# Queries projected transposed, with omega and the norm applied in 64x64 fp32 tiles, in a fused attention and expert layer

## The reference

```python
h = _layernorm(x) * (1 + ca) + sa
q = _heads(h @ wq.T); k = _heads(h @ wk.T); v = _heads(h @ wv.T)
def _phi(x, omega):                       # per head: D = 64 -> M = 64 features
    proj = jnp.einsum('bhnd,md->bhnm', x, omega)
    norm = 0.5 * jnp.sum(x * x, axis=-1, keepdims=True)
    return jnp.exp(proj - norm) / math.sqrt(M)
phi_q = _phi(q, omega); phi_k = _phi(k, omega)
# causal: out = phi_q . cumsum(phi_k v), z = 1 / (phi_q . cumsum(phi_k) + 1e-6)
out = (out * z[..., None]) @ wo.T + bo
...                                       # residual, norm, top-2 routing, experts
```

## Time and profile before

| | us |
|---|---|
| median of 3 executions | 726.92 (726.3 to 727.3) |
| the profiled execution | 727.18 |
| its span in the trace | 725.1 |
| PE busy | 697.4 (96% of the span) |
| DVE busy | 536.0 (74%) |
| ACT busy | 387.6 (53%) |
| POOL busy | 335.6 (46%) |

### The profile page before, as it was taken

One profiled execution on the slowest core, in us unless ns is written; L12 is line 12 of the kernel. 1 busy time (PEld: TensorE's weight loads), 2 busy tenths in 40 slices (PEclk: granted clock), 3 DMA queues, 4 the chain that ended last, 5 costly groups with the idle time before them and its releaser, 6 DMA issues. The chain is left out here.

```text
span 725.1 us, 27349 instructions
## 1 busy us (share of the span) xinstructions
PE 697.4 (96%) x11452; PEld 604.1 (83%) x11452; DVE 536.0 (74%) x1685; ACT 387.6 (53%) x740; POOL 335.6 (46%) x625
## 2 busy tenths in 40 slices
PE   8999999999999999999999999999999789999956
PEld 8788888888888888888888888888887779999942
DVE  6687888878878887888878878888775456565416
ACT  5755566665656665666656566665552144544310
POOL 3002545555544445454545554545447306556550
PEclk9999999999999999999999999999999999999989
DMA  9974000000000000000000000000000154553128
GB/s 252 362 268 178 11 9 11 10 9 11 14 15 10 11 10 11 10 10 11 9 11 11 14 14 9 11 11 11 10 11 14 49 177 130 168 173 113 51 82 304
DMA packets 32705, 47.25 MB, mean 65 GB/s; under 512 B 4132, under 2 KB 20168, under 8 KB 32584
## 3 DMA queue, kind: packets, MB, share of 16 engines
q1 hardware_dynamic: 23296, 32.62, 13.4%
q0 software_dynamic: 4096, 8.42, 3.6%
q10 hardware_dynamic: 5192, 4.47, 1.9%
HBM read 22.21 MB, written 23.36 MB: 63 GB/s over the span
## 5 line engine op out<-in xcount | busy, mean ns | idle before, releaser
L1297 POOL DMA_INDIRECT y_rows<-y_sb,row_id x64 | 62.8, 982 | 66.0 <-DVE y_sb L1442 49.9
L1108 POOL DMA_INDIRECT dispatched<-h_cur,slot x64 | 67.3, 1051 | 17.8 <-issue 16.1
L1376 ACT ACTIVATE hidden<-bank,b_col 128x512 f32<-128x512 f32 x64 | 43.3, 689 | 58.2 <-PE bank L1348 57.8
L632 ACT ACTIVATE phi_k<-expo_k 128x1024 f32<-128x1024 f32 x32 | 33.9, 1058 | 74.5 <-DVE expo_k L768 70.7
L648 ACT COPY v_sb<-bank 128x512 f32<-128x512 f32 x64 | 37.6, 587 | 62.1 <-PE bank L279 58.7
L527 PEld LDWEIGHTS bank<-woT,attT 128*128 128x128 f32 x512 | 61.9, 192 | 3.2 <-ACT attT L738 0.6
L859 DVE TENSOR_TENSOR scores<-bank,within 128x512 f32<-128x512 f32 x64 | 41.2, 686 | 31.2 <-PE bank L310 31.2
L527 PE MATMUL bank<-woT,attT 128*128 128x128 f32 x512 | 62.4, 275 | 0.4 <-ACT attT L738 0.4
L1317 PE MATMUL bank<-w_sb,hidden 128*128 128x128 f32 x512 | 59.7, 275 | 0.8 <-issue 0.8
L137 POOL TENSOR_TENSOR rs<-var,power 128x1 f32<-128x1 f32 x64 | 37.1, 579 | 49.8 <-DVE var L132 49.5
L1317 PEld LDWEIGHTS bank<-w_sb,hidden 128*128 128x128 f32 x512 | 58.3, 192 | 1.2 <-issue 1.2
(11 more groups left out here) (243 smaller groups left out, 2037.9 us busy)
## 6 DMA issues: line engine op xcount, KB each, us to landing
dispatched<-blank SPq DMA_DIRECT2D x16, 524.0 KB, 3.1
region<-dispatched SPq DMA_DIRECT2D x30, 262.0 KB, 2.9
y_rows<-blank SPq DMA_DIRECT2D x8, 512.0 KB, 3.9
w_nat<-in_L_ffn_w_dram SPq DMA_DIRECT2D x8, 256.0 KB, 3.7
y_got<-y_rows SPq DMA_DIRECT2D x8, 256.0 KB, 6.8
y_got<-y_rows ACTq DMA_DIRECT2D x8, 256.0 KB, 7.4
out_dram<-x_sb SPq DMA_DIRECT2D x8, 256.0 KB, 3.7
w_sb<-in_L_ffn_w_dram ACTq DMA_DIRECT2D x6, 256.0 KB, 2.8
```

The source lines that it names most:

```text
L1108: pool.indirect_dma_start(out=dispatched[:, :], in_=h2_cur[par][:], in_offset=None, out_offset=bass.IndirectOffsetOnAxis(ap=slot[par][:, k ...
L1297: pool.indirect_dma_start(out=y_rows[:, :], out_offset=bass.IndirectOffsetOnAxis(ap=row_id[par][:, t:t + 1].bitcast(U32), axis=0), in_=y_s ...
L1376: act.activation(hidden[par][:, k, :], psum[2 + k][:], ACT.Gelu, bias=b1_col[:, bass.ds(e * KH + k, 1)]).then_inc(sem(f"hid{k}_out"), 1)
```

## The change

Queries are projected with the weights stationary and 128 tokens moving, so that the result stands transposed (a head's dimensions on partitions): 24 fp32r matmuls of 128 columns for a chunk in place of 6 of 512. ACT copies this result to `qT` and its square to `qT_square`. PE then multiplies by omega and adds -0.5 times the sum of squares with 32 plain fp32 matmuls of 128 columns in 64x64 tiles (`exponent_qT`), and ACT takes the exponential from PSUM straight into `phiT_q`. Gone are the weights pq, the product of the query weights with omega in the opening, the projection pq, DVE's sum of squares and exponent for the queries, the 8 transposes of `phi_q` and their two copies. The scale of the features is put on the keys' side alone. `minus_half` and `omT` are two small constant tiles. The order of PE's, ACT's and DVE's steps is rewritten.

```diff
+                        def project_qT(half, c, par):
+                            pe.wait_ge(sem(f"pk{half}_out"), times(c + 1))
...
+                            for s in range(4):
+                                o = psum[BANK[f"q{half}"]][:, s * P:(s + 1) * P]
+                                cols = slice(half * 512 + s * P, half * 512 + (s + 1) * P)
+                                pe.matmul(o, wT_hi["q"][:, cols], twice(h_hi[par])[:, toks], start=True, stop=False)
+                                pe.matmul(o, wT_hi["q"][:, cols], h_lo[par][:, toks], start=False, stop=False)
+                                mm = pe.matmul(o, wT_lo["q"][:, cols], twice(h_hi[par])[:, toks], start=False, stop=True)
...
+                        def exponent_qT(c):
+                            for half in range(2):
+                                pe.wait_ge(sem(f"v{half}_out"), c + 2)
+                            for half in range(2):
+                                pe.wait_ge(sem(f"q{half}_out"), c + 2)
...
+                            TERMS = ((omT, qT), (minus_half, qT_square))
+                            for s in range(4):
+                                for n, (w, of) in enumerate(TERMS):
+                                    for side in range(2):
+                                        for r in range(2):
+                                            cols = slice(side * 512 + s * P, side * 512 + (s + 1) * P)
+                                            mm = pe.matmul(psum[BANK[f"pq{r}"]][half_rows(side), s * P:(s + 1) * P],
+                                                           w[half_rows(r), :], of[half_rows(r), cols],
+                                                           start=(n == 0), stop=(n == len(TERMS) - 1), skip_group_check=True)
...
+                        def qT_out(c):
...
+                                act.copy(qT[:, cols], psum[half][:])
+                                act.activation(qT_square[:, cols], psum[half][:], ACT.Square).then_inc(sem(f"q{half}_out"), 1)
...
+                        def exps_q(c, nxt):
...
+                                act.wait_ge(sem(f"pq{r}_in"), c + 2)
+                                act.activation(by_bank[:, r], psum[BANK[f"pq{r}"]][:].rearrange("p (s t) -> p s t", t=P),
+                                               ACT.Exp).then_inc(sem(f"pq{r}_out"), 1)
```

The order of a step on ACT (the names as above), with the old lines out and the new lines in:

```diff
                             if front:
-                                squares("q", c)
+                                qT_out(c)
                             if back:
...
                             if front:
+                                squares_k(c)
                                 values(c, nxt)
                             if last and c != NCH:
                                 rows_out()
+                                logits_out()
                             if live(c, 2):
                                 shift_scale(c, b, j, par)
...
                             if front:
-                                exps("q", c, nxt)
+                                exps_q(c, nxt)
+                            if tail and c != NCH:
+                                heads_out()
```

More of the change, by code:

```diff
@@ L263, in project @@
                         def project(kind, c, par):
[L265 to L268, removed]
+                            w, half = kind[:-1], int(kind[-1])
+                            pe.wait_ge(sem(BEFORE[kind] + "_out"), c + 2)
                             o = psum[BANK[kind]][:]
-                            w, half = kind[:-1], int(kind[-1])
@@ L323, in attend_state @@
                                     pe.wait_ge(sem("lg_out"), c - 1)
+                                if c >= 1:
+                                    for z in range(2):
+                                        pe.wait_ge(sem(f"o{2 + z}_out"), c)
                             else:
@@ L331, in attend_state @@
                                         r = half_rows(z)
[L332 removed]
+                                        mm = pe.matmul(out(i, z, side), phiT_q[par][r, 4 * g + i, half_rows(side)],
                                                        (mid if side else state[par])[r, 4 * g + i, :],
@@ L563, in step @@
                                 pe.wait_ge(sem("h_split"), c + 2)
[L564 to L567, removed]
+                                project_qT(0, c, nxt)
+                                project_qT(1, c, nxt)
+                            features_T(0, c, par)
+                            features_T(1, c, par)
+                            if tail:
+                                attend_state(1, c - 1, nxt, (j - 1) % CPB)
+                                attend(1, c - 1, nxt, (j - 1) % CPB)
                             if front:
@@ L570, in step @@
                                 project("k1", c, nxt)
[L571 to L575, removed]
                             state_gain(0, c, par, j)
-                            if tail:
-                                attend(1, c - 1, nxt, (j - 1) % CPB)
+                            score(0, c, par)
+                            if last:
+                                routing_T(c, par)
                             if front:
@@ L589, in step @@
                                 pe.transpose(psum[BANK["hT"]][:, 0:P], xn[par][:], ident[:]).then_inc(sem("hT_in"), 1)
+                            score(1, c, par)
+                            attend_state(0, c, par, j)
                             if front:
[L591 to L594, removed]
+                                exponent_qT(c)
                             if tail:
@@ L624, in exps @@
[L624 to L632, removed]
+                                cols = slice(half * 512, (half + 1) * 512)
@@ L710, in rows_out, with heads_out @@
                                 act.copy(h2T[:], psum[BANK["h2T"]][:, 0:P]).then_inc(sem("h2T_out"), 1)
+                            def heads_out():
+                                for half in range(2):
+                                    act.wait_ge(sem(f"attT{half}_in"), c)
+                                    act.copy(attT[:, half * 4:half * 4 + 4, :].rearrange("p a b -> p (a b)"),
+                                             psum[BANK[f"attT{half}"]][:]).then_inc(sem(f"attT{half}_out"), 1)
                             def logits_out():
@@ L730, in step @@
                                 rows_out()
+                                logits_out()
                             if live(c, 2):
                                 shift_scale(c, b, j, par)
-                            if last and c != NCH:
-                                logits_out()
-                            if tail:
-                                for half in range(2):
-                                    act.wait_ge(sem(f"attT{half}_in"), c)
-                                    act.copy(attT[:, half * 4:half * 4 + 4, :].rearrange("p a b -> p (a b)"),
-                                             psum[BANK[f"attT{half}"]][:]).then_inc(sem(f"attT{half}_out"), 1)
                             if c == NCH:
+                                heads_out()
                                 rows_out()
```

216 lines of the change are left out of this document (111 added, 105 removed), and 2 rows, old and new, of the table TURNS.

## The result

The changed kernel takes 811.06 us (median of four executions, 805.65 to 814.38) against 727.02: ratio 1.115, interval 1.108 to 1.122, so 84 us slower. Forecast were 791 and a range of 750 to 842. The profiled execution took 808.41, its span is 806.2.

What follows compares the result with a forecast made beforehand. PE's own stream was taken to bound the kernel. Its terms summed to +2.18 us a step, together +64 on the profiled 727.2, giving 791 us; the forecast's own range was 774 to 813, the wider one 750 to 842.

Steps and rivals of the forecast that it cites:

- PE sets the step: Attention: PE's own stream sets the step's length, 16.76 us; ACT and DVE wait for PE.
- The projection, +1.25: Query projection: 24 matmuls each costing a load of 0.11 us, 2.72 against 1.47, so +1.25 us a step.
- loads hidden: Query projection: a load runs beside a stream, a pair costs only its columns, 0.058 us; 752 us, chance 0.10.
- 0.213: Query projection: fp32r loses its pace at 128 columns and costs 0.213 us a matmul; 870 us, chance 0.12.
- one after the other: Query projection: load and stream do not overlap, 0.11 + 0.058 us a pair; 834 us, chance 0.07.
- `exponent_qT`, 1.86: Query exponent on PE: 64 records in 64x64 tiles take 1.70 to 2.01 us a step, taken as 1.86.
- Two at once: Query exponent: its tiles run only two side by side, 0.053 us a record; 839 us, chance 0.04.
- the same whatever the width: Query projection and exponent: every record costs 0.016 us at any column count; 696 us, faster, chance 0.05.
- The gate, +1.0: Gate's matmul: PE stands until ACT has copied the values and then `h2T`, +1.0 us a step.
- The rank's wait for `attT`, +0.2: `routing_rank`: PE waits for ACT's second copy of `attT`, fourth operation behind the exponent, +0.2 us a step.
- DVE's relief at nothing: DVE: the reduction of 1.21 and two operations of 1.32 us taken away count nothing, since PE waits for neither.
- The sum, +64: Whole kernel: +2.18 us a step, 63.2 in 29 steps, plus 2.0, less 0.9, opening 0; together +64 us.

Runs made afterwards that it cites:

- half-column run: The changed kernel with its query projection moving only 64 of the 128 tokens in every step, same 24 loads: 810.96 us.

## Why the prediction was right, point by point

- **PE sets the step.** Shown for what the edits touched: the step moved by what an edit took from PE's stream (1.33 for the projection, 1.12 for the wait), as long as the cover held. At the rank, however, ACT's chain from the exponent on ends last by 0.1 (below).
- **The projection, +1.25.** Measured 2.72 for 2.72, and 1.33 by the run that undoes it. The forecast took the load as the price; the half-column run shows that it is. At 0.111 a pair the rivals "loads hidden" (0.058), "0.213" and "one after the other" (0.168) fall. The Trainium skill's page "TensorE: Matmul & The Clock Gate" lists in "The mechanism" that a load overlaps matmuls in flight only when its row group differs, while a sentence ahead of that list also allows a load into a background weight buffer. The trace does not agree with the list, by the 0.111 for the 0.168; into which buffer the loads go no run shows. The 81 ns for a load and a matmul of 128 columns that the Trainium skill gives on the same page ("Back-to-back issue gap") are below the 111 ns measured.
- **`exponent_qT`, 1.86.** In the opening of the changed kernel it runs by itself, 8 records every 0.22, so 0.0272 each and 1.75 in all, near the bound of four tiles side by side. "Two at once" and "the same whatever the width" fall.

```profile
23.38 0.40 PE L297 MATMUL bank<-qT_square,minus_half 64*64 64x128 f32 x8
23.60 0.40 PE L297 MATMUL bank<-qT,omT 64*64 64x128 f32 x8
```

- **The gate, +1.0.** 1.01 in the step shown (342.83 - 341.59 is 1.24, of which a matmul takes 0.23), 1.12 by the run that removes it. No line of the diff names this term: it comes from where a copy and a matmul now stand.
- **The rank's wait for `attT`, +0.2.** There, at half the size, 0.1, though PE's list of waits does not show it. ACT's second copy of `attT` ends at 348.30 (347.22 + 1.08) and the rank starts at 348.36, 0.06 behind it; the same 0.06 stands in 28 of the 29 steps. `attend` ahead of the rank takes 0.67 (from 347.69) where the bare one takes 0.58. So up to the rank ACT's chain and PE's stream are nearly even, and PE alone would have little to gain there.
- **DVE's relief at nothing.** Right in the sum, since none of the 29 steps waits for `hot`, but its reason was too simple. The relief is worth 0.5 a step in the changed kernel, since without it `hot` would come late for the rank. The text had the cover (4.5 against 3.6 us), and the 3.6 already left out the 1.32 of `expo_q`: with it 4.9, by its own numbers 0.4 late. In the trace `hot` ends at 347.68 and the rank starts at 348.36, 0.7 later.
- **The sum, +64.** It is 81 between the profiled executions, 84 between the medians: near the upper end of the forecast's own range of 774 to 813. That it lies inside is in part luck: that range was made of the exponent, the loads and the waits, and much of the shortfall comes from elsewhere. The step was sized 2.18 and measured 2.53, which makes 10 us in 29 steps. The step shown, 19.13 against 16.76, has 2.37 of it. The transposes that went save 0.77 there, not 0.87: the sixteen before took 0.79 and 0.97 with one entry to the tiles, in the lines below, and the eight that are left take 0.99 with one entry (335.18 to 336.17).

```profile
326.21 0.60 PE L296 MATMUL bank<-ident,phi_q 128*128 128x128 f32 x4
...
327.00 0.47 PE L277 MATMUL bank<-wk_hi,h_hi 128*128 128x512 f32 x1
...
328.47 0.60 PE L296 MATMUL bank<-ident,phi_q 128*128 128x128 f32 x4
...
329.44 0.27 PE L332 MATMUL bank<-state,phiT_q 64*64 64x65 f32 x2
```

`attend_state` and the exponent together take 2.32 (343.83 to 346.15), 1.80 more than the 0.52 of `attend_state` alone and 0.06 under the term. What is left, 2.37 - 1.25 + 1.47 + 0.77 - 1.80 = 1.56 for the gate, the tile shapes and the rank, was put at 1.41. The other 0.16 of the mean lie outside the steps shown: the mean after is 0.13 longer than the step shown, the mean before 0.03 shorter. The opening was put at 0 and the first steps at 2.0; together they took 4.7. The last step was put at -0.9 and took 2.4 more: 1.0 with the lower clock level in that execution (13.26 against 12.26), 0.8 since the transpose now reaches PE before POOL has its rows (by the run that puts it back), and 0.6 that no run explains.

## What to carry to other kernels

Turning a projection round to save a transposition multiplies the loads of weights, here 24 for 6; where the stream is shorter than the load, as at 128 columns here, the count of loads is the price, and halving the columns saves nothing. An order written by hand is part of a change: read each wait of each engine against what now stands ahead of it, here a 0.27 us copy behind two value copies that cost 34 us. And work taken off an engine with idle time may still be holding a deadline: look at how long before its consumer it ends, not only at its busy share.

## What the runs showed of the hardware

PE's granted clock fell to the lower level within a projection of 48 matmuls of 64 columns, after 3.7 us of it, while PE was busy without a gap; this happened in 19 of that run's 32 projections. With 24 matmuls, of 128 columns or of 64, it stayed up in the 29 steps counted, but in an early step of the half-column run it fell at 32.3, right behind 24 matmuls of 64 columns (29.27 to 31.95), again with PE busy. The load costs 0.111 us at the upper level and 0.213 at the lower one, so it follows the clock as the columns do: in that early step a matmul of 512 columns at the lower level takes 0.43 (34.30 to 34.73) where 0.23 is usual.
